# Differential attention with a soft mixture of experts: the middle stage written out, transposes in pairs

## The reference

```python
q = (xn @ Wq).reshape(B, S, 2, h, dh)      # h = 16 heads of dh = 64, two sets; k and v alike
s1 = einsum('bshd,bthd->bhst', q1, k1) * scale    # causal; s2 from q2, k2
o = einsum(a1, v1) - lam * einsum(a2, v2)         # a = softmax(s)
attn = (o.reshape(B, S, h * dh) * 0.2) @ Wo
logits = (einsum('tzd,ed->tze', x, phi_w) + phi_b).reshape(t, z, 64, 32)
D = softmax(logits, axis=3); C = softmax(logits, axis=2)
X_tilde = einsum('tznp,tzd->npd', D, x)           # then clip, norm, tanh, one 128x128 expert each
Y = einsum('tznp,npH->tzH', C, Y_tilde)
```

## Time and profile before

| | us |
|---|---|
| median of 3 runs (1450.42 to 1450.93) | 1450.45 |
| the profiled execution | 1451.76 |
| its span, first to last instruction | 1449.9 |
| TensorE busy | 1358.3 (94%) |
| ScalarE busy | 1152.2 (79%) |
| POOL busy | 1131.3 (78%) |
| VectorE busy | 1082.6 (75%) |

### The profile page before, as it was taken

The page is one execution under the profiler, slowest core; times in us unless marked ns, Lnnn a source line. Parts: engine busy times, 40 slices in busy tenths (PEclk is TensorE's granted clock), DMA queues, the critical chain, the costliest instruction groups (busy, mean ns, idle before and its releaser), DMA issues. The chain is left out here.

```text
span 1449.9 us, 31521 instructions
## 1 busy us (share of the span) xinstructions
PE 1358.3 (94%) x9298; PEld 1035.1 (71%) x9425; DVE 1082.6 (75%) x2235; ACT 1152.2 (79%) x3354; POOL 1131.3 (78%) x878
## 2 busy tenths in 40 slices
PE   3899999999999999999999999899999996699998
PEld 2677777767777677777776777677777774588886
DVE  6678877787778777877787778777787786655554
ACT  4778888877888788878887888788888885699997
POOL 2468788888888788878887888788888888299997
PEclk9999999999999999999999999999999998799999
DMA  5111011101111111111111111111101100600101
GB/s 165 46 38 36 32 47 38 37 34 48 38 36 36 48 38 36 36 49 38 36 36 49 38 36 35 41 38 39 38 25 37 38 17 5 158 16 15 30 15 30
DMA packets 64462, 59.59 MB, mean 41 GB/s; under 512 B 17536, under 2 KB 45200, under 8 KB 64144
## 3 DMA queue, kind: packets, MB, share of 16 engines
q1 hardware_dynamic: 60608, 55.86, 12.0%
q10 hardware_dynamic: 3664, 1.44, 0.4%
HBM read 15.34 MB, written 2.10 MB: 12 GB/s over the span
## 5 line engine op out<-in xcount | busy, mean ns | idle before, releaser
L687 ACT ACTIVATE e<-ps_s,neg_max 128x256 f32<-128x256 f32 (+1 forms) x1024 | 415.2, 431 | 126.8 <-DVE neg_max L762 126.8
L762 DVE TENSOR_REDUCE neg_max<-ps_s 128x2 f32<-128x512 f32 (+1 forms) x384 | 241.4, 684 | 153.2 <-PE ps_s L545 153.2
L911 POOL TENSOR_TENSOR disp<-logit,gmax 128x512 f32<-128x512 f32 x128 | 135.1, 1056 | 261.6 <-DVE gmax L806 224.8
L674 ACT ACTIVATE pT<-ps_t 128x512 f32<-128x512 f32 x384 | 237.9, 621 | 67.3 <-PE ps_t L520 66.2
L919 POOL TENSOR_TENSOR e<-e,inv 128x1024 f32<-128x1024 f32 x128 | 279.6, 2184 | 0.0
L520 PEld LDWEIGHTS ps_t<-ident,e 128*128 128x128 f32 x1536 | 185.9, 140 | 91.8 <-issue 71.6
L520 PE MATMUL ps_t<-ident,e 128*128 128x128 f32 x1536 | 230.2, 273 | 5.8 <-issue 4.6
L687 ACT ACTIVATION_READ_ACCUMULATOR e<-ps_s,neg_max 128x1 f32 x1024 | 221.8, 217 | 0.0
L545 PE MATMUL ps_s<-qk 64*128 64x256 f32 (+1 forms) x2048 | 202.4, 337 | 18.5
L545 PEld LDWEIGHTS ps_s<-qk 64*128 64x128 f32 x2048 | 172.7, 186 | 44.6 <-issue 40.6
L1164 POOL TENSOR_TENSOR c_lo<-cT,c_hi 128x512 fp32r<-128x512 f32 x128 | 166.4, 1302 | 40.0 <-ACT cT L1207 29.7
(11 more groups left out here) (148 smaller groups left out, 3110.8 us busy)
## 6 DMA issues: line engine op xcount, KB each, us to landing
xs<-xT SPq DMA_DIRECT2D x128, 256.0 KB, 2.4
fx<-xT SPq DMA_DIRECT2D x64, 64.0 KB, 1.9
fxn<-xn SPq DMA_DIRECT2D x32, 64.0 KB, 1.9
xres<-in_L_attn_x SPq DMA_DIRECT2D x8, 256.0 KB, 3.1
out_dram<-res SPq DMA_DIRECT2D x8, 256.0 KB, 2.4
xn<-in_L_attn_x SPq DMA_DIRECT2D x2, 512.0 KB, 6.7
xn<-in_L_attn_x ACTq DMA_DIRECT2D x2, 512.0 KB, 7.9
bias<-in_L_ffn_phi_b SPq DMA_DIRECT2D x1, 1024.0 KB, 6.7
```

The costliest lines, as they stand in the source:

```text
L674: nc.scalar.activation(pT[:, k, :], ps_t[:, (q + k) % 2, :], ACT.Copy).then_inc(t_out, 1)
L687: ins = nc.scalar.activation(dst, ps_s[:, k, i * width:(i + 1) * width], ACT.Exp, bias=neg_max[:, q, c:c + 1], accum_out=total[:, q, c:c + 1])
L762: nc.vector.tensor_reduce(neg_max[:, q, c:c + heads], ps_s[:, k, :].rearrange("p (h t) -> p h t", h=heads), AX.X, ALU.max, negate=True).th ...
L911: nc.gpsimd.tensor_tensor(by_expert(bank_of(disp, t, jj)), by_expert(bank_of(logit, t, jj)), gmax[:, jj, :].unsqueeze(2).to_broadcast([P, ...
```

## The change

The main stage is written out in full: `run` calls `step` for all iterations with plain numbers, so there is no loop, no back-edge, no register; `carry_wait` with `spare`, and `first_tile`, are gone. At the head of each step on TensorE the second block of transposes moves up behind the first; in an odd step projections 0 and 1 follow, in an even one both halves of the values. ScalarE copies in the same order in even steps. On VectorE `values_low` and `output_low` move from the head of step 3 to behind `slot_max`.

```diff
-        def run(eng, step):
-            for it in range(PER):
-                for j in range(4):
-                    step(it, j, 0, it)
-            with eng.Fori(1, NG - 1) as g:
-                for kk in range(PER):
-                    for j in range(4):
-                        step(PER * g + kk, j, g, kk)
-            for it in range(ITER - PER, ITER + 2):
+        def run(step):
+            for it in range(ITER + 2):
                 for j in range(4):
                     step(it, j, it // PER, it % PER)
...
                     turn(0)
+                    turn(1)
                     qk_part(0)
-                    turn(1)
                     qk_part(1)
                     turn(2)
                     qk_part(2)
                     qk_part(3)
                 else:
                     turn(0)
+                    turn(1)
                     if live(unit, NU):
                         make_v(unit, (j // 2) % 2, g, 0, use["v0"])
-                    turn(1)
                     if live(unit, NU):
                         make_v(unit, (j // 2) % 2, g, 1, use["v1"])
                     turn(2)
...
                     transposed_out(v - 2, j % 2, 0)
+                    transposed_out(v - 2, j % 2, 1)
                     take_v(unit, j, 0)
-                    transposed_out(v - 2, j % 2, 1)
                     take_v(unit, j, 1)
                     transposed_out(v - 2, j % 2, 2)
...
-            def carry_wait(c, j):
-                nc.vector.memset(spare[:, 4 * c + j:4 * c + j + 1], 0.0)
...
                 inverse(v - 1, (j + 1) % 2)
-                if live(g + 1, NG) and (kk, j) == (PER - 1, 3):
-                    values_low(nc, dve, env, g + 1)
-                if live(g, NG) and (kk, j) == (0, 3) and not (isinstance(g, int) and g == 0):
-                    output_low(nc, dve, env, g)
                 if j % 2 == 1:
                     next_queries(it, j, 0)
                     dispatch_sum(*back(it, j, 2))
                     next_queries(it, j, 1)
                     dispatch_inverse(*back(it, j, 2))
                     slot_max(*back(it, j, 1))
+                    if live(g + 1, NG) and (kk, j) == (PER - 1, 3):
+                        values_low(nc, dve, env, g + 1)
+                    if live(g, NG) and (kk, j) == (0, 3) and g > 0:
+                        output_low(nc, dve, env, g)
```

More of the change, by code:

```diff
@@ L58, in wait @@
 def wait(eng, sem, value):
-    if isinstance(value, int) and value <= 0:
-        return
-    eng.wait_ge(sem, value)
+    if value > 0:
+        eng.wait_ge(sem, value)
 def live(i, n):
-    return not isinstance(i, int) or 0 <= i < n
+    return 0 <= i < n
 def f32(ap):
@@ L386, in main_phase @@
         m_run = sb("m_run", [P, BK])
-        spare = sb("spare", [P, 20])
         ps_tu, ps_s, ps_t, ps_o = psum("ps_tu", 2), psum("ps_s", 3), psum("ps_t", 2), psum("ps_o", 1)
@@ L418, in bank_of @@
         def bank_of(buf, t, j):
-            return buf[:, bass.ds((t % 2) * NS_ + j * BK, BK)]
+            return buf[:, (t % 2) * NS_ + j * BK:(t % 2) * NS_ + (j + 1) * BK]
         def by_expert(ap):
@@ L458, in load_xs @@
                 for h in range(2):
-                    sp.dma_start(f32(xs[q][h][:]), f32(xT[h][:, bass.ds(pair * PT, PT)])).then_inc(xs_in[q], 16)
+                    sp.dma_start(f32(xs[q][h][:]), f32(xT[h][:, pair * PT:(pair + 1) * PT])).then_inc(xs_in[q], 16)
             def load_tile(it):
@@ L467, in load_tile @@
                     for h in range(2):
-                        sp.dma_start(f32(fx[h][:]), f32(xT[h][:, bass.ds((it + 1) * P, P)])).then_inc(fx_in, 16)
+                        sp.dma_start(f32(fx[h][:]), f32(xT[h][:, (it + 1) * P:(it + 2) * P])).then_inc(fx_in, 16)
                 if live(it, NTT):
-                    sp.dma_start(fxn[:], x_sb[:].rearrange("p t d -> p (t d)")[:, bass.ds(it * D, D)]
+                    sp.dma_start(fxn[:], x_sb[:, it, :]
                                  ).then_inc(fxn_in, 16)
@@ L485, in iteration @@
                 load_tile(it)
[L487 to L493, removed]
+            for it in range(ITER):
+                iteration(it, it % PER, it // PER)
         @block.tensor
@@ L624, in step @@
                 use = BANKS[j]
-                if j == 0 and kk == 0 and not (isinstance(g, int) and g == 0):
-                    last_use[BANKS[3]["lg"]] = (lg_out, 4 * it)
-                    last_use[BANKS[3]["xt"]] = (xt_out, 4 * (it - 1))
                 def turn(k):
@@ L665, in _ @@
                 project(0, 0, 0, i, i % 2)
-            run(pe, step)
+            run(step)
         @block.scalar
@@ L740, in step @@
                     values_high(nc, act, env, g + 1)
-                if live(g, NG) and (kk, j) == (0, 2) and not (isinstance(g, int) and g == 0):
+                if live(g, NG) and (kk, j) == (0, 2) and g > 0:
                     act.wait_ge(wo_mm, NPAIR * g)
@@ L746, in _ @@
                 take_keys(0, 0, i, i % 2)
-            run(act, step)
+            run(step)
         @block.vector
         def _(dve):
-            def carry_wait(c, j):
-                nc.vector.memset(spare[:, 4 * c + j:4 * c + j + 1], 0.0)
             def bank_max(v, j):
@@ L789, in take_logits @@
             def take_logits(t, j):
-                if isinstance(t, int) and t == 0 and j == 0:
+                if t == 0 and j == 0:
                     dve.wait_ge(bias_in, 16)
@@ L876, in step @@
                         wait(dve, wo_out, unit - 2)
-                        o = o_acc[:, bass.ds(((unit - 2) % NPAIR) * PT, PT)]
+                        o = o_acc[:, ((unit - 2) % NPAIR) * PT:((unit - 2) % NPAIR + 1) * PT]
                         nc.vector.tensor_tensor(o, ps_tu[:, BANKS[j]["wo"], :], o, ALU.add).then_inc(wo_out, 1)
@@ L894, in _ @@
                 take_queries(0, 0, i, i % 2)
-            run(dve, step)
+            run(step)
         @block.gpsimd
         def _(pool):
-            def first_tile():
-                pool.wait_ge(fx_in, 32)
             def step(it, j, g, kk):
@@ L906, in step @@
                 if live(t, NTT):
-                    first_tile()
                     pool.wait_ge(g_done, 4 * t + jj + 1)
@@ L938, in step @@
                 if live(t, NTT):
-                    first_tile()
                     pool.wait_ge(m_done, t + 1)
                     bank = by_expert(bank_of(logit, t, jj))
-                    nc.gpsimd.tensor_tensor(bank, bank, m_all[:, bass.ds(t * NP_, NP_)].unsqueeze(1)
+                    nc.gpsimd.tensor_tensor(bank, bank, m_all[:, t * NP_:(t + 1) * NP_].unsqueeze(1)
                                             .to_broadcast([P, EB, NP_]), ALU.subtract).then_inc(c_sub, 1)
-            run(pool, step)
+            run(step)
 def experts_phase(nc, env):
```

8 lines of the change are left out of this document (2 added, 6 removed).

## The result

| us | before | after |
|---|---|---|
| median | 1450.69 (4 runs, 1450.42 to 1451.85) | 1473.39 (4 runs, 1473.00 to 1473.74) |
| the profiled execution, its span | 1451.76, 1449.9 | 1473.74, 1471.9 |
| VectorE busy | 1082.6 | 1138.2 |
| TensorE busy | 1358.3 | 1372.9 |

The changed kernel is slower: ratio 1.0155, 95% interval 1.0137 to 1.0172, or 22.7 us. 1475 was forecast, 24.7 us above before. The mean granted clock of the two profiled executions is nearly the same (0.988 before, 0.987 after), so the difference is one of waits.

What follows compares the result with a forecast made beforehand. TensorE was taken to bound the middle stage. 17.4 + 6.0 + 4.4 + 6.0 + 14.7 - 23.8 = +24.7 us on the profiled 1451.76 gave 1476.5; with the median 1.3 lower, 1475 us, range 1454 to 1488.

Steps and rivals of the forecast that it cites:

- likeliest case: The forecast itself, all costs and the gain as summed: 1475 us, own range 1463 to 1485, chance 0.55.
- b, behind the rounding: Seven even steps where ScalarE first rounds projections: output product 0.63 us later each, +4.4 us.
- c, output split: Step 3, seven times: one split waits for POOL's next operation, score maxima 0.85 us late, +6.0 us.
- c, value splits: Step 3, seven times: two splits wait for two POOL operations, score maxima 2.1 us late, +14.7 us.
- loop and early splits: Middle stage: removing five back-edges and the group boundaries' early splits saves all 23.8 us.
- Cost a: Odd steps: the fourth projection waits 0.28 us more for VectorE's second copy of queries, 62 times, +17.4 us.
- the two banks cover the pair: Rival, odd steps: alternating banks hide the copy, so the fourth projection waits no longer; 1458 us, chance 0.06.
- Cost b: Even steps: the output product waits 0.11 us for V0's later copy, 55 times, +6.0 us, plus 4.4 behind the rounding.
- Cost c: Step 3: splits behind the running maximum wait for POOL's operations, +6.0 us (output) and +14.7 us (values).
- the split costs little: Rival, step 3: VectorE keeps its turn or the maximum gets in first, splits cost 3 us in all; 1457 us, chance 0.15.
- Late work spreads: Rival: late VectorE also holds V0 through the logits' copy and POOL goes out of step; +10, 1485 us, chance 0.12.
- Faster: Rival: heads covered in both kinds of step, splits fit into idle time; -20, 1430 us, chance 0.12.

Runs made afterwards that it cites:

- e1: The kernel before, only written out without the loop, all orders as before: 1436.96 us.
- e7: The changed kernel with VectorE's sum of the mixture behind both copies of queries instead of between them: 1454.99 us.
- e12: The changed kernel with each later group's split replaced by a VectorE reduction of the same 128 columns, for timing only: 1453.57 us.
- e6: The changed kernel with the later groups' value and output splits on POOL, at the end of its step 3: 1453.03 us.
- e10: e9 with the changed kernel's TensorE heads (paired transposes), ScalarE's old order of copies: 1420.41 us.
- e2: e1 with the value and output splits moved behind the running maximum: 1434.78 us.
- e4: e1 with the pair of transposes in even steps only, on TensorE and ScalarE: 1444.44 us.
- e8: The changed kernel with ScalarE copying V0 before the second block of transposes again, TensorE's order as changed: 1457.99 us.
- e9: e1 with the splits on POOL and, in VectorE's odd steps, both query copies and running maximum ahead of the mixture's sum and inverse: 1424.27 us.
- e5: The changed kernel with each later group's split replaced by a one-input VectorE multiply by zero, for timing only: 1470.98 us.

## Why the prediction was right

**The sum.** 1475 against 1473.4, by the likeliest case and its mechanisms. By its terms:

| term | forecast | measured |
|---|---|---|
| a, the fourth projection waits for the copy of queries | 62 x 0.28 = 17.4 | 0.29 a step (9.67 for 9.38): 18.0 |
| b, the output product waits for V0's copy | 55 x 0.11 = 6.0 | 0.10 a step: 5.5 |
| b, behind the rounding | 7 x 0.63 = 4.4 | 9.24 for an ordinary even step of 8.62: 4.3 |
| c, output split | 7 x 0.85 = 6.0 | 0.75 a step: 5.3 |
| c, value splits | 7 x 2.1 = 14.7 | 2.05 a step: 14.4 |
| loop and early splits | -23.8 | the rest of 22.7: -24.8 |

- *Gain.* e1 gives 13.7 us for the loop, so about 10 are left for the early splits. e1's ordinary iteration is 35.95 us, not the 36.01 from which the 23.8 were counted, so writing out gave some 1.5 us that the sum did not have. One reading under this term does not carry what it is used for: the 1.16 and 1.21 us between the copies of queries were to show that the memsets cost nothing, but the step of the earlier trace rows has the memset as well (a row of 0.06 us at 62.75, beside the sum). The changed kernel has none, and its two copies stand 1.21 us apart too; so the conclusion holds.
- *Cost a* held to 0.01 us because both ends were counted: the copy chain of iteration 0 and TensorE's own row. The rival in which the two banks cover the pair falls: P0 to P3 alternate over two banks in after as before, and P3 waits. Here the rotation covered a copy only where as much work stood between as the chain of copies took. e7 shows what was not seen: the wait was not 0.28 but 0.41 us from a step without any, since before already paid a part (below).
- *Cost b* held, and its bound of 0.15 was not reached.
- *Cost c* was the most extrapolated term, and its size was off by about a tenth in one part (0.75 for 0.85 us) and less in the other. The maximum missed its turn by 0.16 us in the trace; the forecast's own h + 3.73 and h + 3.58 give 0.15, which its rival rounds to 0.1. The rival "the split costs little" falls with the rows of step 3, and e12 and e6 show that the turns, not the arithmetic, are the cost. That each split costs a whole POOL operation, because the two engines take turns, is read from the rows alone.
- *Late work spreads*, the 1485 us rival: its first half is there, in the row L76 <- DVE logit L776 (V0 held by the copy of the logits, up to 1.7 us). It adds nothing, because the output product waits longer still for ScalarE, and POOL's row was back in step one step later (its first subtraction starts at h + 3.49 in step 0 of iteration 16, and at h + 1.56, as in ordinary steps, in step 1). So it has its mechanism and not its price.
- *Faster* falls with all of a, b and c. Yet each cost can be taken away, and then the same pairs run in the fastest kernel tried (e10).

One reason was incomplete: the costs were added as independent. They are not (e2 to e4: 12 us of interaction in the thirty; e8: some 5 us more than b). The sum came out because cost c was worked out with the maximum already put late by cost a, and with no slack left at V0.

## What to carry to other kernels

Before moving two blocks of TensorE work together, count from one timeline how long the copy that frees the bank takes from the start of the last product, and how much work is left between that product and the bank's next user; that the banks alternate says nothing about that. When two engines take turns, as VectorE and POOL do here, the order of asking can matter more than the work: 0.3 us of lateness put one VectorE operation behind POOL's longest, and each small operation behind it cost another whole POOL operation. Putting such small operations on the engine that they would wait for took the whole cost away here (e6), though in e9 and e10 a part came back, 0.8 and 0.4 us at the next head. On VectorE only two places were tried, the head of the step and behind the running maximum. Take the costs of a combined edit one at a time before judging any part: here the pairs cost nothing once the copies that they wait for were early enough.

## What the runs showed of the hardware

- **A fourth projection that waits costs some 0.1 us beyond its wait.** In step 3 of the changed kernel the waiting product lasts 0.50 and the next one starts 0.34 later; in e7, where nothing waits, it lasts 0.40 and the next starts 0.23 later, at h + 3.41 (the changed kernel, then e7):

```profile
551.58 0.50 PE L76 MATMUL ps_tu<-xs,a_w 128*128 128x512 f32 x1
551.92 0.40 PE L77 MATMUL ps_tu<-xs,a_w 128*128 128x512 f32 x1
...
171.80 0.40 PE L76 MATMUL ps_tu<-xs,a_w 128*128 128x512 f32 x1
172.03 0.39 PE L77 MATMUL ps_tu<-xs,a_w 128*128 128x512 f32 x1
```

  The kernel before starts it at h + 3.42 and has the row of 0.50 us: a hardly visible wait of 0.01 us, and 0.1 for it in most odd steps. That is where e7, e9 and e10 have odd steps of 9.26 instead of 9.38. The rows do not show what the 0.1 us is.
- **A one-input multiply from SBUF to SBUF takes turns with POOL like a two-input operation; a reduction does not.** 128 columns: median 1.19 us for the 14 multiplies of e5 that stand for value splits, against 0.27 for the 14 reductions of e12 in the same place.
- **A back-edge costs its own step 1.8 to 2.8 us** (10.77 to 11.40 us before; in e1 8.61 or 8.62, and 8.97 at the first). Taking out all five is worth 13.7 us; what is left of that, some 0.5 a back-edge, lies in the steps behind it and in the ordinary iterations.
